# Cross-attention kernel on one core: second attention begun inside the batch loop, first stage reordered, unread products on TensorE

## The chip, the cores and the metric

The kernel runs on one core of a Trainium2 chip. Its time is the device time of one execution in microseconds (us). Three executions of the kernel before took 262.43, 263.16 and 263.74 us; their median, 263.16, is the time before. A profiled execution was recorded apart from them.

## What is computed

```python
# stage 0: only batch 0 matters (its attention is added to every batch)
q, k, v = x[0] @ Wq.T, ctx[0] @ Wk.T, ctx[0] @ Wv.T      # 256 tokens, 256 features, 16 heads of 16
tgt2 = softmax(q k^T / 4) v                               # per head
y = x + tgt2                                              # x: (32, 256, 256)
# stage 1: for each of 32 batches
nF, nX = layernorm(y) * w2 + b2, layernorm(ctx) * w1 + b1
attended = softmax(nF nX^T / 16) nX
h = gelu(attended @ fc1.T + fc1_b)                        # 4 hidden features
cross = h @ fc2.T + fc2_b
nc = layernorm(cross) * w3 + b3
self = softmax(nc nc^T / 16) nc                           # the second attention
out = nF + gamma2 * (cross + gamma1 * self)
```

## The kernel before

There are no helpers of a compiler here: each engine has its own hand-written program (functions under `@block.tensor`, `vector`, `scalar`, `gpsimd`, `sync`), and semaphores tie them together. So an instruction that waits holds back everything behind it on its engine, and the order of the lines is the order of the work.

**First attention** (VectorE L301 to L416, ScalarE L700 to L724, TensorE L811 to L903). 16 heads are done as eight pairs, `p = 0..7`. Per pair TensorE writes scores for two heads into two of four banks (L865), VectorE takes row maxima (L380), ScalarE four exponentials (L718), TensorE transposes them into banks 5 and 6 (L881), ScalarE copies bank 5 (L724) and VectorE bank 6 (L386), and every second pair TensorE multiplies with the values (L894). In the same loop VectorE takes the statistics of the first six context batches and, at `p = 6` and `p = 7`, sets the padding of `sU` to zero (L400, two memsets) and cuts the output operand in three bf16 parts (`output_operand`, L330, four chained instructions).

**Joint.** VectorE adds tgt2 to batches 0 and 1 (L468), GpSimd to all later ones (L615, `add`). Statistics (L351), then a reciprocal root on GpSimd (L622) and the normalization: y on VectorE (L371), context on GpSimd (L635).

**Loop over 32 batches** `b` (TensorE L965 on). Per batch: transposes of a later pair (`turned`, L852) into banks 3, 4, 2 in turn, evacuated by ScalarE into `XT` and `Fall` (L735, L738); scores of batch b (L915); maxima (L488); two exponentials (L762); transposes of the weights of b - 1 (L923), which ScalarE copies into PT (L756). Every four batches, a projection of the context to the four hidden features (L935), turned by way of a copy on VectorE (vT, L514) and L943, and the product of weights and values (`apply`, L953), turned back by way of oTq (VectorE, L522) and L961 (`apply_back`), saved in OA (L525). DMA loads run on one queue (SP), four pairs ahead.

**Algebra** (`algebra(g, part)`, L434). For each half `g` of the tokens (32 columns) VectorE runs a chain in which each instruction waits for the one before (`link`): reciprocal and bias, products with a 5 x 5 form and a reduction (L447), a reciprocal root by three Newton steps (L430 to L432), products with a 6 x 6 form (L460), and a cut into bf16 parts (L287 to L290). GpSimd cuts the other side (`right`, L667 to L675). `LATE` says after which batch each part of half 0 runs, `NEXT` after which iteration of the second attention each part of half 1 runs:

```python
LATE = {26: (0,), 29: (1,), 30: (2,), 31: (3,), 32: (4,), 33: (5,)}
NEXT = {0: (0,), 2: (1,), 3: (2, 3), 4: (4,), 5: (5,)}
```

The VectorE and TensorE loops run to b = 35; the steps behind batch 31 are the last transposed weights, `apply(7)` and `apply_back(7)`, and on VectorE the last parts of the algebra.

**Second attention** (TensorE L1077 on): 16 pairs of batches, `p = 0..15`, in a pipeline of 21 iterations. `turn(p)` (L1001) transposes both cut sides into bank 4; ScalarE copies it for even p (L775), VectorE for odd p (L542). `scores(p)` (L1012); VectorE takes maxima of two batches (L535); these are turned (L1023), copied by ScalarE (L781) and subtracted by TensorE (`shift`, L1031); ScalarE takes exponentials (L787). At even p: `attend` (16 products, L1044), `output_turn` (L1063); at odd p `back` (L1053). VectorE copies the result (L548), saves it (OB, L553), and GpSimd cuts it (L681 to L688). From p = 5 on, `output(p - 5)` (L1073) writes banks 6 and 7 and VectorE adds them to `Fall` (`finish`, L564); a pair of batches is then stored (SP, L270). The next `output` waits for that addition.

## Time and profile before

| | us |
|---|---|
| median of three executions | 263.16 (262.43 to 263.74) |
| the profiled execution, whole | 262.2 |
| its span, first to last instruction | 260.4 |
| busy: TensorE / weight loads | 213.0 / 143.4 |
| busy: VectorE | 207.4 |
| busy: ScalarE | 140.9 |
| busy: GpSimd | 125.4 |
| mean granted TensorE clock (share of full speed) | 0.854 |
| first attention | 0 to about 42 |
| loop over the batches | about 50 to 174 |
| second attention and output | about 178 to 260 |

Engines in the rows: PE is TensorE (PEld its weight loads, which overlap), DVE is VectorE, ACT ScalarE, POOL GpSimd, SP the engine that issues the DMAs. A row of the timeline gives the start, the duration, the engine and line, what is written and read, and how many instructions are merged; in brackets the idle time before it and what ended it. A busy TensorE may still be far from its peak, as its instructions overlap. The clock of TensorE has two levels, 2.4 GHz (1.00) and 1.2 GHz (0.50). The 16 pairs of stores end 3.2 us after the last addition.

### The profile page before, as it was taken

Reading aid. Unit: us, or ns where it says so; the run is one execution under the profiler, and the core shown is the slowest. Engines: PE = TensorE matmul, PEld = TensorE weight load, DVE = VectorE, ACT = ScalarE, POOL = GpSimd, SP = SyncE. Lnnn points to the kernel's source line nnn. Section 1 sums busy time; section 2 is a strip of 40 time slices with the busy share of each in tenths; the row PEclk is TensorE's granted clock in tenths of the full one; section 3 lists DMA queues with packets and bytes.
Section 4 is the critical chain, followed back from the end, with each engine's and each line's share of the span. In section 5 each row is a group of like instructions: output and inputs, shape, how many; then the busy total and the mean of one; then the engine's idle time right before and its main releaser. Section 6 shows DMA issues by size and latency. Waiting matters only on the chain.

```text
span 260.4 us, 4676 instructions
## 1 busy us (share of the span) xinstructions
PE 213.0 (82%) x1614; PEld 143.4 (55%) x1614; DVE 207.4 (80%) x413; ACT 140.9 (54%) x260; POOL 125.4 (48%) x186
## 2 busy tenths in 40 slices
PE   3989868289999999999999999963786568888731
PEld 3856535267778778796988789632222223333210
DVE  5678886999999989888998953886569958988663
ACT  1066764216677778586776778840564335454300
POOL 6000087677999979999697840041003512222220
PEclk9999999659999999999999999985555557777865
DMA  5980000044444425355450000000000024333556
GB/s 185 363 302 3 1 1 3 0 161 161 165 161 142 144 95 156 114 164 162 159 166 0 4 0 3 0 0 3 1 0 1 0 83 162 141 144 125 204 198 242
DMA packets 14711, 26.80 MB, mean 103 GB/s; under 512 B 1760, under 2 KB 1760, under 8 KB 14688
## 3 DMA queue, kind: packets, MB, share of 16 engines
q1 hardware_dynamic: 14688, 26.50, 29.2%
q8 instruction: 13, 0.21, 0.3%
q14 instruction: 10, 0.08, 0.1%
HBM read 18.11 MB, written 8.39 MB: 102 GB/s over the span
## 4 chain that ended last, share of the span: by engine, by line
PE 59%; DVE 24%; ACT 6%; issue 6%; POOL 2%; DMA 1%; SPq 0%; POOLq 0%; DVEq 0%; ACTq 0%
PE psum L915 17%; PE psum L852 8%; PE psum L923 5%; PE psum L1044 4%; DVE xN L371 4%; DVE nm L535 3%; DVE bn L351 3%; PE psum L953 3%; PE psum L822 2%; PE psum L935 2%; PE psum L1012 2%; DVE Fall L564 2%; PE psum L1073 2%; PE psum L865 2%; PE psum L881 2%
## 5 line engine op out<-in xcount | busy, mean ns | idle before, releaser
L915 PE MATMUL psum<-XT,Fall 128*128 128x256 f32 x256 | 62.6, 388 | 1.1 <-ACT Fall L738 1.1
L915 PEld LDWEIGHTS psum<-XT,Fall 128*128 128x128 f32 x256 | 47.2, 195 | 7.1 <-ACT Fall L738 1.7
L615 POOL TENSOR_TENSOR xN<-xN,tgt 128x512 f32<-128x512 f32 x30 | 39.1, 1306 | 1.5 <-DVE tgt L415 1.5
L635 POOL TENSOR_SCALAR cN<-cN,nmean,rstd 128x256 f32<-128x256 f32 x64 | 36.4, 579 | 2.4 <-POOL rstd L622 2.3
L371 DVE TENSOR_SCALAR xN<-xN,bn,rstd 128x256 f32<-128x256 f32 x64 | 34.8, 586 | 1.1 <-POOL rstd L622 1.1
L756 ACT ACTIVATE PT<-psum 128x512 f32<-128x512 f32 x32 | 19.1, 598 | 28.6 <-PE psum L923 28.6
L488 DVE TENSOR_REDUCE nmax<-psum 128x2 f32<-128x512 f32 x32 | 21.9, 684 | 12.6 <-PE psum L915 12.4
L622 POOL TENSOR_TENSOR rstd<-vps,minus_half 128x8 f32<-128x8 f32 (+1 forms) x16 | 24.8, 1549 | 13.8 <-DVE vps L362 13.8
L762 ACT ACTIVATE E<-psum,nmax 128x256 f32<-128x256 f32 x64 | 26.7, 473 | 8.3 <-DVE nmax L488 8.2
L681 POOL CAST sC<-co 128x160 bf16<-128x160 f32 x8 | 2.5, 317 | 53.9 <-DVE co L558 53.9
L738 ACT ACTIVATE Fall<-psum,par 128x512 f32<-128x512 f32 x32 | 23.4, 792 | 4.8 <-PE psum L852 4.7
L564 DVE TENSOR_TENSOR Fall<-psum,Fall 128x1024 f32<-128x1024 f32 x16 | 19.5, 1221 | 7.6 <-PE psum L1073 7.6
L735 ACT ACTIVATE XT<-psum,b1s,w1s 128x512 f32<-128x512 f32 x32 | 23.0, 788 | 3.7 <-PE psum L852 3.7
L535 DVE TENSOR_REDUCE nm<-psum 128x4 bf16<-128x1024 f32 x16 | 19.5, 1218 | 4.5 <-PE psum L1012 4.3
L351 DVE BATCH_NORM_STATS2 bn<-cN 128x6 f32<-128x512 f32 x32 | 22.2, 693 | 0.0
L852 PE MATMUL psum<-ident,xN 128*128 128x128 f32 x128 | 18.2, 289 | 4.7 <-DVE xN L371 4.7
L351 DVE BATCH_NORM_STATS2 bn<-xN 128x6 f32<-128x512 f32 x32 | 21.9, 685 | 0.0
L923 PE MATMUL psum<-ident,E 128*128 128x128 f32 x128 | 20.2, 280 | 1.6 <-ACT E L762 1.6
L787 ACT ACTIVATE PT<-psum 128x1024 f32<-128x1024 f32 x16 | 16.4, 1022 | 9.2 <-PE psum L1031 9.1
L923 PEld LDWEIGHTS psum<-ident,E 128*128 128x128 f32 x128 | 14.3, 141 | 9.6 <-issue 6.5
L852 PEld LDWEIGHTS psum<-ident,xN 128*128 128x128 f32 x128 | 15.7, 150 | 5.5 <-issue 5.1
L852 PE MATMUL psum<-ident,cN 128*128 128x128 f32 x128 | 17.1, 274 | 0.1
(156 smaller groups left out, 337.0 us busy)
## 6 DMA issues: line engine op xcount, KB each, us to landing
cN<-ctx SPq DMA_DIRECT2D x32, 256.0 KB, 2.9
xN<-x SPq DMA_DIRECT2D x32, 256.0 KB, 4.1
out<-Fall SPq DMA_DIRECT2D x32, 256.0 KB, 2.3
x0T<-x0t SPq DMA_DIRECT2D x1, 256.0 KB, 2.7
wqT<-wqt SPq DMA_DIRECT2D x1, 256.0 KB, 3.3
c0T<-c0t SPq DMA_DIRECT2D x1, 256.0 KB, 4.0
wkT<-wkt SPq DMA_DIRECT2D x1, 256.0 KB, 5.0
wvT<-wvt SPq DMA_DIRECT2D x1, 256.0 KB, 5.2
```

The costliest lines, as they stand in the source:

```text
L351: dve.bn_stats(bn[:, (b // 2) % 4, side, b % 2, :], src[:, b % SLOTS, :].rearrange("p (t d) -> p d t", t=NT)).then_inc(st_ok, 1)
L371: dve.tensor_scalar(own, own, stat(p, 1, m, t, 1), root_of(p, 1, m, t), ALU.subtract, ALU.mult)\
L535: dve.tensor_reduce(nm2[:, p % 2, :, 0:NT], scored(p).rearrange("p (m t k) -> p m t k", m=2, t=NT), AX.X, ALU.max, negate=True).then_inc(m ...
L564: dve.tensor_tensor(own, psum[:, 6 * 512:8 * 512], own, ALU.add).then_inc(fin_ok, 1)
L615: pool.tensor_tensor(xN[:, b % SLOTS, :], xN[:, b % SLOTS, :], tgt2[:, :, :].rearrange("p t d -> p (t d)"), ALU.add).then_inc(y_ok, 1)
L622: pool.tensor_tensor(rstd[:, p % 4, sides, :].rearrange("p s k -> p (s k)"), vps[:, p % 4, sides, :].rearrange("p s k -> p (s k)"), minus_ ...
L635: pool.tensor_scalar(own, own, nmean[:, p % 4, NT * m + t:NT * m + t + 1], root_of(p, 0, m, t), ALU.add, ALU.mult)\
L738: act.activation(Fall[:, 2 * p:2 * p + 2, c, :], tiles(own), ACT.Identity, bias=c_("b2", c), scale=c_("w2", c)).then_inc(evac_ok, 1)
L762: act.activation(E[:, b % 2, t * N:(t + 1) * N], bank[SBANK1[b % 3]][:, t * N:(t + 1) * N], ACT.Exp, bias=nmax[:, b % 2, t:t + 1]).then_in ...
L852: last = pe.transpose(bank[TBANK[n % 3]][:, m * N + t * P:m * N + (t + 1) * P], z[:, (2 * p + m) % SLOTS, t * D + c * P:t * D + (c + 1) * ...
L915: last = pe.matmul(bank[SBANK1[b % 3]][:, t * N:(t + 1) * N], Fall[:, b, c, t * P:(t + 1) * P], XT[:, p % 4, c, m * N:(m + 1) * N], start= ...
L923: last = pe.transpose(bank[SBANK1[b % 3]][:, k * N + t * P:k * N + (t + 1) * P], E[:, b % 2, t * N + k * P:t * N + (k + 1) * P], ident[:, :])
```

## The change

It does nine things.

1. The two memsets of `sU` go from `p = 6` of the first attention to the very start of VectorE's program, with a semaphore of their own.
2. The cuts of the output operand: part 1 goes behind the copies of Q and K, part 2 from `p = 7` to batch 18 of the loop.
3. ScalarE copies bank 5 (weights of the pair before) between the exponentials of the first and those of the second head, and TensorE waits for each half of the copies apart.
4. The additions of tgt2 to batches 2 and 3 go from GpSimd to VectorE, so VectorE does the first four; GpSimd starts its own at batch 4 and waits until VectorE has normalized batches 0 and 1.
5. In the loop the copies vT and oTq go from VectorE to ScalarE.
6. The algebra of half 0 is split in nine parts and runs in batches 20 to 29; the transposes `turn(0)`, `turn(1)` and `scores(0)` run in TensorE's batches 30 and 31. `apply(7)`, `apply_back(7)` and the saving of OA run inside iteration 0 of the second attention.
7. ScalarE makes all copies sT, even and odd.
8. `output(13)` and `output(15)` write to banks 2, 3 and 0, 1, which the scores no longer need. All additions stay on VectorE: the tuple `ASIDE`, which would send some by way of ScalarE to GpSimd, is empty, and the code around it makes no instructions.
9. `keep_busy(n, b)`: n products of the identity with itself, 128 columns wide, into a bank that is written anew before it is read. Seven at the start, eleven behind the first six context transposes, four and three around the last weights, then five behind each `shift` up to p = 4 and two from p = 5 on.

```diff
-LATE = {26: (0,), 29: (1,), 30: (2,), 31: (3,), 32: (4,), 33: (5,)}
-NEXT = {0: (0,), 2: (1,), 3: (2, 3), 4: (4,), 5: (5,)}
+LATE = {20: (0,), 22: (1,), 23: (2,), 24: (3,), 25: (4,), 26: (5,), 27: (6,), 28: (7,), 29: (8,)}
+NEXT = {0: (0,), 2: (1, 2), 3: (3, 4), 4: (5, 6), 5: (7, 8)}
+ASIDE = ()
...
+    def result(n):
+        return {13: (2, 3), 15: (0, 1)}.get(n, (6, 7))
...
+        for side in range(2):
+            dve.memset(sU[:, side, :, SU:SLOT], 0.0).then_inc(pads_ok, 1)
...
-        output_operand(1)
...
+        output_operand(1)
...
-                if p == 2 * EARLY:
-                    for side in range(2):
-                        dve.memset(sU[:, side, :, SU:SLOT], 0.0).then_inc(zero_ok, 1)
-                elif p > 2 * EARLY:
-                    output_operand(2)
...
+                dve.wait_ge(zero_ok, 6)
+                products(ha[:, G, :], Q[:, :], H + 1)
+            elif part == 2:
+                link(dve.tensor_reduce(w5, produced(H + 1), AX.X, ALU.add))
+            elif part == 3:
...
+            elif part == 4:
...
+            elif part == 5:
+                products(u[:, G, :], K[:, :], U)
+            elif part == 6:
+                link(dve.tensor_reduce(uK[:, G, :], produced(U), AX.X, ALU.add))
+            elif part == 7:
+                left_cut(uK[:, G, :], cut[:, G, 0:U], sU[:, 0, G, :], U)
...
-                left_cuts(uK[:, G, :], cut[:, G, 0:U], sU[:, 0, G, :], U)
+                left_rest(cut[:, G, 0:U], sU[:, 0, G, :], U)
...
+        def add(b):
...
+        add(0)
+        add(1)
...
-        statistics(2, 1)
+        add(2)
+        add(3)
...
+        statistics(2, 1)
...
+        def saved(q):
+            dve.wait_ge(ob_mm, q + 1)
+            dve.tensor_copy(OA[:, q, :, :, :], by_batch(bank[7][:, 0:N], H + 1)).then_inc(o_saved, 1)
+        for b in range(B):
...
-            if b % 4 == 1 and q < QUADS:
-                dve.wait_ge(vt_mm, q + 1)
-                if q >= 1:
-                    dve.wait_ge(vb_mm, q)
-                dve.tensor_copy(vT[:, :], bank[6][:, 0:N]).then_inc(vT_ok, 1)
+            maximum(b)
...
-                    dve.wait_ge(oq_mm, q)
-                    if q >= 2:
-                        dve.wait_ge(ob_mm, q - 1)
-                    dve.tensor_copy(oTq[:, :], bank[7][:, 0:N]).then_inc(oTq_ok, 1)
+                values(q)
...
-                dve.wait_ge(ob_mm, q)
-                dve.tensor_copy(OA[:, q - 1, :, :, :], by_batch(bank[7][:, 0:N], H + 1)).then_inc(o_saved, 1)
+                saved(q - 1)
...
+            if b == 18:
+                output_operand(2)
...
-        def turned(p):
-            dve.wait_ge(st_mm, p + 1)
-            if p >= 2:
-                dve.wait_ge(s2_mm, p - 1)
-            dve.tensor_copy(sT[:, 1, :], bank[4][:, 0:NT * P].bitcast(BF16)).then_inc(sT_ok[1], 1)
...
+            dve.tensor_tensor(pair(n), results(n), pair(n), ALU.add).then_inc(fin_ok, 1)
...
-        turned(1)
+        saved(QUADS - 1)
...
-            if p % 2 == 1 and p + 2 < PAIRS:
-                turned(p + 2)
...
-            if b == 2:
+            if b == 4:
...
+                pool.wait_ge(zy_ok, 4)
...
-        add(2)
-        add(3)
...
+                if m == 0 and p >= 1:
+                    act.wait_ge(p0_mm, 2 * p - 1)
+                    if p >= 4:
+                        act.wait_ge(o0_mm, (p - 4) // 2 + 1)
+                    act.activation(PT[:, 2 * ((p - 1) % 3), :], bank[5][:, :], ACT.Copy).then_inc(pt0_ok[0], 1)
+            if p == 5:
+                act.wait_ge(o0_mm, NHP // 4)
+                act.activation(oT[:, 0, :], bank[0][:, :], ACT.Copy).then_inc(oT_ok[0], 1)
...
-            if b == 28:
-                hidden(0)
...
+        def turned_values(q):
+            act.wait_ge(vt_mm, q + 1)
+            if q >= 1:
+                act.wait_ge(vb_mm, q)
+            act.activation(vT[:, :], bank[6][:, 0:N], ACT.Copy).then_inc(vT_ok, 1)
+        def applied(q):
+            act.wait_ge(oq_mm, q + 1)
+            if q >= 1:
+                act.wait_ge(ob_mm, q)
+            act.activation(oTq[:, :], bank[7][:, 0:N], ACT.Copy).then_inc(oTq_ok, 1)
...
+            act.activation(sT[:, p % 2, :], bank[4][:, 0:NT * P].bitcast(BF16), ACT.Copy).then_inc(sT_ok[p % 2], 1)
...
+            if b >= 1:
+                weights_copied(b - 1)
+            exponentials(b)
+            if b % 4 == 1:
+                turned_values(q)
+            if b % 4 == 2 and q >= 1:
+                applied(q - 1)
+            if b == 21:
+                hidden(0)
+            if b == 29:
+                act.wait_ge(r_mm, 1)
+                act.activation(RT[:, :], bank[4][:, 0:DC * P // 2].bitcast(BF16), ACT.Copy).then_inc(rt_ok, 1)
+            if b == 30:
+                turned(0)
+        weights_copied(B - 1)
+        turned(1)
...
+            if p == 0:
+                applied(QUADS - 1)
+            if p + 2 < PAIRS:
...
+        def keep_busy(n, b):
+            for _ in range(n):
+                pe.matmul(bank[b][:, 0:P], ident[:, :], ident[:, :], start=True, stop=True)
+        pe.wait_ge(consts, 4)
+        keep_busy(7, 4)
...
-                if p >= 2:
-                    pe.wait_ge(pt0_ok[0], p - 1)
-                    pe.wait_ge(pt0_ok[1], p - 1)
...
+                    if p >= 2:
+                        pe.wait_ge(pt0_ok[m], p - 1)
...
+        keep_busy(11, 7)
...
+            if p == 0:
+                pe.wait_ge(rt_ok, 1)
+                pe.wait_ge(pads_ok, 2)
+                pe.wait_ge(alg, ALG["left", 0])
+                pe.wait_ge(right_ok, 6)
+                pe.wait_ge(zero_ok, 6)
...
-            if p >= 2:
+            if p == 0:
+                pe.wait_ge(evac_ok, 4 * PAIRS)
+            elif p == 1:
+                pe.wait_ge(PT_ok, B)
+            else:
...
+            if n == 14:
+                pe.wait_ge(fin_ok, own_adds(13))
+            elif n in (13, 15):
+                pe.wait_ge(exp2_ok, PAIRS)
...
+            elif n >= 1:
+                pe.wait_ge(fin_ok, own_adds(n))
...
-        pe.wait_ge(alg, ALG["left", 0])
-        pe.wait_ge(right_ok, 6)
-        pe.wait_ge(zero_ok, 8)
-        pe.wait_ge(PT_ok, B)
-        pe.wait_ge(rt_ok, 1)
-        turn(0)
-        scores(0)
-        turn(1)
...
+            if b == 31:
+                scores(0)
+            if b == B:
+                pe.wait_ge(V1_ok, QUADS)
+                keep_busy(4, 6)
...
+            if b == 30:
+                turn(0)
+            if b == 31:
+                turn(1)
...
+            if p == 0:
+                keep_busy(3, 6)
+                apply(QUADS - 1)
...
+            if p == 0:
+                apply_back(QUADS - 1)
...
+                keep_busy(5 if p < 5 else 2, 5)
```

## Rows read from the trace of the kernel before

**Rows 1.** Windows: length, busy PE, PEld, DVE, ACT, POOL, granted clock, DMA share, GB/s.
```profile
110.00:120.00 10.00, 10.00 (x76) 8.35 (x75) 8.77 (x21) 7.59 (x15) 9.19 (x10) 1.00 0.56 175
160.00:170.00 10.00, 9.79 (x79) 7.17 (x78) 6.56 (x16) 8.34 (x16) 0.00 (x0) 1.00 0.01 2
200.00:210.00 10.00, 5.44 (x40) 1.84 (x32) 9.62 (x18) 2.41 (x5) 5.45 (x11) 0.50 0.05 20
230.00:240.00 10.00, 8.05 (x79) 3.09 (x81) 8.69 (x16) 5.18 (x9) 2.50 (x9) 0.79 0.42 157
```

**Rows 2.** Timeline, first attention (start, us, engine, line, [idle before]); last, the last score.
```profile
4.92 3.78 PE L822 MATMUL psum<-x0T,wqT 128*128 128x256 f32 x8 [0.47 <-DMA wqT<-wqt]
...
9.19 0.18 DVE L288 TENSOR_TENSOR Rcut<-Rt,stR 128x20 f32<-128x20 f32 x1
...
28.17 1.09 PE L881 MATMUL psum<-ident,E 128*128 128x128 f32 x8 [0.79 <-ACT PT L724]
...
33.55 1.74 DVE L400 MEMSET sU<- 128x896 uint32 x2
...
34.21 1.09 PE L881 MATMUL psum<-ident,E 128*128 128x128 f32 x8 [0.80 <-ACT PT L724]
...
37.16 0.45 DVE L288 TENSOR_TENSOR Rcut<-Rt,stR 128x20 f32<-128x20 f32 x1
...
168.49 1.95 PE L915 MATMUL psum<-XT,Fall 128*128 128x256 f32 x8
```

**Rows 3.** Timeline, joint between first attention and loop, and three rows from inside the loop.
```profile
43.78 2.37 DVE L468 TENSOR_TENSOR xN<-xN,tgt 128x512 f32<-128x512 f32 x2
...
48.71 2.31 DVE L371 TENSOR_SCALAR xN<-xN,bn,rstd 128x256 f32<-128x256 f32 x4 [0.54 <-POOL rstd L622]
...
130.34 1.27 POOL L615 TENSOR_TENSOR xN<-xN,tgt 128x512 f32<-128x512 f32 x1
...
135.07 0.72 DVE L371 TENSOR_SCALAR xN<-xN,bn,rstd 128x256 f32<-128x256 f32 x2
...
139.07 1.87 DVE L371 TENSOR_SCALAR xN<-xN,bn,rstd 128x256 f32<-128x256 f32 x2
```

**Rows 4.** Timeline, end of the loop: exponentials, transposes, products of the algebra.
```profile
143.07 0.84 ACT L762 ACTIVATE E<-psum,nmax 128x256 f32<-128x256 f32 x2
...
144.95 0.60 PE L923 MATMUL psum<-ident,E 128*128 128x128 f32 x4
...
164.38 0.98 DVE L424 TENSOR_TENSOR kv<-ha,Q 128x800 f32<-128x800 f32 x1
```

**Rows 5.** Window of four batches inside the loop.
```profile
118.46:133.30 14.84, 14.84 (x120) 12.12 (x124) 12.99 (x28) 10.65 (x21) 12.26 (x15) 1.00 0.44 144
```

**Rows 6.** Timeline, head of the second attention.
```profile
178.31 0.29 PEld L961 LDWEIGHTS psum<-ident,oTq 128*128 128x128 f32 x2 [3.91 <-DVE oTq L522]
...
180.77 1.23 DVE L535 TENSOR_REDUCE nm<-psum 128x4 bf16<-128x1024 f32 x1 [1.53 <-PE psum L1012]
...
185.98 1.23 DVE L535 TENSOR_REDUCE nm<-psum 128x4 bf16<-128x1024 f32 x1 [0.81 <-PE psum L1012]
```

**Rows 7.** Timeline, two iterations of the second attention, and late value products.
```profile
230.66 0.41 DVE L542 COPY sT<-psum 128x512 bf16<-128x512 bf16 x1
...
232.50 1.89 PE L1044 MATMUL psum<-PT,u 128*6 128x256 f32 x16
...
239.47 1.89 PE L1044 MATMUL psum<-PT,u 128*6 128x256 f32 x16
...
244.56 1.05 PE L1044 MATMUL psum<-PT,u 128*6 128x256 f32 x16 [0.31 <-ACT PT L787]
```

**Rows 8.** Window of 2 us inside an odd iteration.
```profile
230.00:232.00 2.00, 1.12 (x15) 0.54 (x13) 1.93 (x6) 1.09 (x2) 0.28 (x2) 1.00 0.70 262
```

**Rows 9.** Timeline, the last two additions.
```profile
254.00 1.22 DVE L564 TENSOR_TENSOR Fall<-psum,Fall 128x1024 f32<-128x1024 f32 x1 [0.79 <-PE psum L1073]
...
256.02 1.23 DVE L564 TENSOR_TENSOR Fall<-psum,Fall 128x1024 f32<-128x1024 f32 x1 [0.80 <-PE psum L1073]
```

More of the change, by code:

```diff
@@ L237, in score_bank, with own_adds, results, aside @@
         return bank[2 * (1 - p % 2) + m]
+    def own_adds(n):
+        return sum(i not in ASIDE for i in range(n))
+    STORED = tuple(range(PAIRS))
+    def result(n):
+        return {13: (2, 3), 15: (0, 1)}.get(n, (6, 7))
+    def results(n):
+        a, _ = result(n)
+        return psum[:, 512 * a:512 * (a + 2)]
+    def aside(n):
+        return XT[:, (n // 2) % 2, :, :].rearrange("p c n -> p (c n)")
+    def pair(n):
+        return Fall[:, 2 * n:2 * n + 2, :, :].rearrange("p b c n -> p (b c n)")
     TURNS = [(p, 0) for p in range(EARLY)] + [(p, 1) for p in range(EARLY)] \
@@ L454, in algebra @@
                 newton(v, y, t)
-            elif part == 3:
+            elif part == 4:
                 newton(v, y, t)
@@ L576, in _ @@
                 returned((p - 3) // 2)
-            if p >= 5:
+            if p >= 5 and p - 5 not in ASIDE:
                 finish(p - 5)
@@ L688, in output_cuts, with add_aside @@
             pool.tensor_tensor(to[:, :, 2 * CO:3 * CO], left, to[:, :, CO:2 * CO], ALU.subtract).then_inc(sC_ok, 1)
+        def add_aside(n):
+            pool.wait_ge(aside_ok, ASIDE.index(n) + 1)
+            pool.tensor_tensor(pair(n), aside(n), pair(n), ALU.add).then_inc(added_ok, 1)
         right(0)
@@ L695, in _ @@
                 output_cuts((p - 3) // 2)
+            if p - 5 in ASIDE:
+                add_aside(p - 5)
     @block.scalar
@@ L707, in _ @@
         for p in range(NHP + 1):
[L708 to L712 removed]
+            for m in range(2):
+                if p < NHP:
                     act.wait_ge(max0_ok, 2 * p + m + 1)
@@ L794, in output_turned, with set_aside @@
             act.activation(cT[:, q % 2, :], bank[4][:, 0:NT * P].bitcast(BF16), ACT.Copy).then_inc(cT_ok, 1)
-        turned(0)
-        for p in range(2 * QUADS + 3):
+        def set_aside(n):
+            act.wait_ge(f_mm, n + 1)
+            if ASIDE.index(n) >= 2:
+                act.wait_ge(added_ok, ASIDE.index(n) - 1)
+            act.activation(aside(n), results(n), ACT.Copy).then_inc(aside_ok, 1)
+        for p in range(2 * QUADS + 4):
             if p < PAIRS:
                 maxima_turned(p)
-            if p % 2 == 0 and p + 2 < PAIRS:
+            if p == 0:
+                applied(QUADS - 1)
+            if p + 2 < PAIRS:
                 turned(p + 2)
@@ L803, in _ @@
                 weights(p)
+            if p - 5 in ASIDE:
+                set_aside(p - 5)
             if p == 1:
@@ L1072, in output @@
                     rows = slice(SLOT * m, SLOT * m + SC)
-                    last = pe.matmul(bank[6 + m][:, c * N:(c + 1) * N], RT[rows, c * P:(c + 1) * P],
+                    last = pe.matmul(bank[result(n)[m]][:, c * N:(c + 1) * N], RT[rows, c * P:(c + 1) * P],
                                      cT[rows, (n // 2) % 2, (n % 2) * N:(n % 2 + 1) * N], start=True, stop=True)
             last.then_inc(f_mm, 1)
-        pe.wait_ge(alg, ALG["left", 0])
-        pe.wait_ge(right_ok, 6)
-        pe.wait_ge(zero_ok, 8)
-        pe.wait_ge(PT_ok, B)
-        pe.wait_ge(rt_ok, 1)
-        turn(0)
-        scores(0)
-        turn(1)
+        for b in range(B + 1):
+            k, m, q = b // 2, b % 2, b // 4
+            if k + 1 < PAIRS and (m == 1 or k + 1 >= EARLY):
+                turned(k + 1, m)
+            if b < B:
+                score(b)
+            if b % 4 == 1 and q < QUADS:
+                project(q)
+            if b % 4 == 2:
+                project_back(q)
+                if q >= 1:
+                    apply(q - 1)
+            if b % 4 == 3 and q >= 1:
+                apply_back(q - 1)
+            if b == 31:
[3 more added lines that the diff above has]
+                keep_busy(4, 6)
+            if b >= 1:
+                weights_turned(b - 1)
+            if b == 29:
+                pe.wait_ge(evac_ok, 62)
+                pe.wait_ge(alg, ALG["stR"])
+                for c in range(DC):
+                    last = pe.transpose(bank[4][:, c * P // 2:(c + 1) * P // 2].bitcast(BF16),
+                                        stR[:, c, :, :].rearrange("p m r -> p (m r)"), identb[:, :])
+                last.then_inc(r_mm, 1)
+            if b == 30:
+                turn(0)
+            if b == 31:
+                turn(1)
         for p in range(2 * QUADS + 5):
```

124 lines of the change are left out of this document (41 added, 83 removed).

## The prediction

> **What bounds the kernel now.** I read the stretches first, then each joint between stages in the timeline. The stretches [rows 1] show three regimes. Inside the loop (58 to 170 us) TensorE is busy 9.8 to 10.0 of every 10 us at full clock (2.4 GHz), so there only work on TensorE, or an engine that falls behind it, moves the end. From 200 to 210 us it is busy 5.44 of 10 at a granted clock of 0.50 (1.2 GHz), and VectorE 9.62: latencies and VectorE set the pace. After 214 us the clock alternates between its levels (mean 0.79 from 230 to 240). Ahead of the loop the time goes in chains between engines.
>
> **Start and first attention.** The 16 projection products (8 then 8) run on the path: the first eight took 3.78 us, while eight such products took 1.95 in the loop [rows 2]. The change puts seven unread products in front. If that brings the full clock 1.5 us earlier the second set gains most of 1 us, if not nothing. Ends 0 and 1.8; I take 0.7, as the first set still runs cold.
> The two memsets (33.55 to 35.29) hold back a row maximum whose scores were finished before they began; at VectorE's start they lie in its wait for the parameters [rows 2]. Gain 1.7.
> ScalarE copied half of the turned weights after all four exponentials; TensorE's transposes at 34.21 waited 0.80 for that copy [rows 2]. Two iterations last 34.21 - 28.17 = 6.04 [rows 2]: transposes 1.1, value products 1.0, scores 1.1, first maximum 0.7, exponentials 1.57, copy 0.5. With the copy before the second pair and the two waits split, the first transposes hide behind the second exponentials: about 0.4 less per two iterations, 3.5 times, 1.4. Ends 0 and 2. The operand cuts moved to batch 18 gain nothing here (VectorE then waited anyway); those put behind K fit the wait for the first scores.
>
> **Joint to the loop.** Two additions go from GpSimd to VectorE, two instructions more there. But VectorE's own two took 2.37 us while GpSimd added, and its four normalizations 2.31 beside another GpSimd addition; two normalizations beside a GpSimd power took 0.72, beside additions 1.87 [rows 3]. With GpSimd made to wait for the first four normalizations I count: additions 1.2 (gain 1.2), two more additions 1.2 that fill the wait for the root, normalizations 1.45 (gain 0.9). About 2.0, and 0.3 from the first score, which ran at half clock and may run warm after eleven unread products. Gain 2.3; ends 1 and 3.5. First stage and joint: 6.1.
>
> **Loop.** The algebra of the first half moves from batches 26 to 33, where VectorE was busy 6.56 of 10 us [rows 1], to 20 to 29, and a cut to batch 18. Up to batch 25: cuts 0.85, reciprocal and bias 1.0, products 1.0 [rows 4], reduction 1.0, eight small instructions 2.0, seven more 1.7: 7.5 us. VectorE is busy 12.99 of the 14.84 us of four batches [rows 5], idle 1.9, so 3.8 in eight, and the copies of vT and oTq (0.42 each, four of them) leave it: 5.5. Exponentials were ready at 143.9 for transposes at 144.95 [rows 4], elsewhere 2 us ahead: a maximum may come some 1.5 us later. That leaves 0.5 us of stall if the moved instructions keep their length. They lose their quiet neighbour, though: GpSimd was at 0 between 160 and 170 us, and works 9.2 of 10 here [rows 1]. A cut beside GpSimd's normalizations took 0.45, like two of its neighbours, and the same one beside an idle GpSimd 0.18 [rows 2]: +0.3 each. Some 21 of the moved ones are of kinds that would meet it; GpSimd's powers do not disturb (0.72 above) and are a fifth of its time, so I take 0.2 each, 4.2. Stall 4.7, ends 0 and 10; with the turn of pair 0 now ahead of the last score, 0.35: a loss of 5.0. ScalarE takes the 0.42 copies with room (7.59 of 10 busy) [rows 1]. Its two table loads for Gelu only move from batch 28 to 21.
>
> The Trainium skill (SBUF — State Buffer, Who interferes with whom) says that a VectorE instruction with two SBUF inputs and a GpSimd instruction that reads SBUF exclude each other for the whole instruction. By it each would wait out the rest of a GpSimd addition (1.27 long [rows 3]), not a part of 0.3; that is the third rival below.
>
> **Head of the second attention.** Before, the last score ended at 170.4; then came the last weights, the last value products, the cuts, and maxima(0) at 180.77, maxima(2) at 185.98: 15.6 us after it [rows 2, 6]. Between lay a wait of 3.91 of TensorE's queue for a copy (L522) that stood behind the algebra on VectorE. After, by the same durations from the end T of the last score: scores(0) T+0.5, maxima(0) T+1.0, last exponentials T+2.0 (they queue behind one copy on ScalarE), their copy T+4.1, last value products T+4.2 to 5.2, back T+5.8, OA saved T+6.4, maxima(1) T+7.6, weights(0) T+8.1, maxima(2) T+8.7. VectorE now waits for OA before maxima(1), and every turned(p) queues on ScalarE between two others. Gain 15.6 - 8.7 = 6.9; half clock would cost 1.4 of it. From p=3 to p=6 VectorE runs without a gap (algebra of the second half, same instructions), so each odd turned() that leaves it (0.41, some 0.33 in the chain) counts: p=1, 3, 5, 7, 1.4 in all. At p=6 the path goes through TensorE: value products 1.89 cold, 1.05 warm [rows 7], 0.8 less. Gain 6.9 + 1.4 + 0.8 = 9.1.
> The unread products cost some 0.12 us each (half of a 256-column product, 1.95 / 8 [rows 2]), cold twice that. I count those of the head (four and three) and the five an iteration up to p=4 at nothing: TensorE waits there for exponentials, for a copy or for a maximum, 1 us or more. Without that cover they are 0.6 to 1.2 an iteration, and TensorE itself is late next.
>
> **Steady part, p=8 to 15.** Two iterations take 7.0 us (232.50 to 239.47) [rows 7]: finish 1.1, maximum 1.15, turned 0.33, OB copied 0.3, then TensorE from the maxima's transpose to the output, 4.1. Without turned: -0.33. TensorE's part holds the 16 value products (1.89 at 1.2 GHz, 1.05 at 2.4) and two sets of four (some 0.2 each): 1.2 less if the clock stays up, and two unread products more, 0.25 warm or 0.5 cold. So per pair of iterations between +0.1 and -1.1 (VectorE's own 5.9 us is the floor). The granted clock was 0.79 here before [rows 1]: full in the odd iterations, where TensorE was busy 1.1 of 2 us [rows 8], and down again after them. I take -0.6, four times: 2.4. Ends 0 and 4.4.
>
> **End.** The last three additions stood 2.02 apart: addition (1.23), output products that wait for it, addition. With other banks for two of them they follow each other in 1.23, the last transfer as before 3.2 after it: 2 x 0.8 = 1.6 [rows 9], less 0.2 as the transfers, 2 us a pair, close up. Gain 1.4. All other additions stay where they are: ASIDE is empty, so the aside code makes nothing.
>
> **Sum.** -6.1 + 5.0 - 9.1 - 2.4 - 1.4 = -14.0. The profiled execution took 262.2 (span 260.4), so 248.2; the runs' median, 263.16, is 1.0 above that execution, so 249. A measurement of this kernel tells about 0.5% (1.3 us) from no change.
>
> **Rivals.**
> *Clock and cover both hold*: TensorE stays at 2.4 GHz through the second attention and VectorE keeps up. The loop loses 1.4 and not 5.0, the steady part gives 4.4, the start 1.8: 6.7 less, 242. For it: unread products fill gaps like that of [rows 8]. Against: from p=5 on they are only two, 0.25 us in some 3. 0.2.
> *The clock does not hold and VectorE lags*: head loses 1.4, p=6 0.8, steady gives 0, loop 10 instead of 5, start 0: 10.3 more, 258 to 259; half of it 254. For it: from 200 to 210 us the clock stayed at 0.50 though TensorE was busy 5.44 of 10 [rows 1]. 0.22 for 252 to 259.
> *Slower than before*: the moved algebra, batches 18 to 25, each of 21 instructions waiting out a whole GpSimd addition of 1.27: 7.5 + 27 - 5.5 - 1.5 = 27 of stall instead of 4.7, 271. It turns slower from 0.9 us per instruction on. Against: the cuts that met GpSimd paid 0.3. 0.04.
> *It does not begin in the loop*: turn(0) waits for the cuts of either engine. GpSimd's (4.2 us, after its last normalization at 152.7) and VectorE's (end in batch 29) are both ready before batch 30, but a lag of VectorE of over 4 us would move them: the head's 6.9 shrink to 3, 253. 0.04.
> My forecast, a small stall and a clock that alternates: 0.5.
>
> **Range and chances.** The own ends of the terms give 240 to 259; holding 8 in 10 and leaving out the slower case and the worst of the second rival, 242.5 to 256. Faster by over 0.5%: 0.93; within: 0.03; slower: 0.04.
>
> **What would show it.** Right: no memset before a maximum in the first attention; VectorE's first additions at about 0.6 each; maxima(0) about 1 us after the last score and maxima(2) under 9; last additions 1.23 apart. The loop step is right if the batches 22 to 26 show TensorE waiting for exponentials and VectorE's small instructions at 0.3 to 0.5; wrong if TensorE stays at 10.00 there, or if it stalls over 10. The clock step is wrong if the steady cycle stays near 6.7 or falls to 5.9. The whole is wrong if the loop loses what the head gains.

## The result and the profile after

The changed kernel takes 246.95 us (median of four executions, 246.19 to 247.89); the kernel before took 263.45 (262.43 to 263.82) beside it. The ratio is 0.938, with a 95% interval from 0.934 to 0.942. The profiled execution took 246.86, its span is 245.1 and the mean granted clock 0.957 (before: 262.2, 260.4, 0.854).

The windows of the changed kernel (columns as in [rows 1]), first those that answer to [rows 1], then the two that differ most:

```profile
110.00:120.00 10.00, 10.00 (x88) 7.76 (x87) 8.31 (x18) 6.69 (x14) 9.64 (x11) 1.00 0.33 112
160.00:170.00 10.00, 9.75 (x84) 7.19 (x76) 3.49 (x8) 5.40 (x14) 0.00 (x0) 1.00 0.01 2
230.00:240.00 10.00, 5.04 (x50) 1.97 (x46) 6.90 (x12) 1.19 (x2) 3.00 (x10) 0.70 0.56 210
...
190.00:200.00 10.00, 5.05 (x37) 2.54 (x38) 9.53 (x14) 2.79 (x6) 5.20 (x11) 0.65 0.15 54
200.00:210.00 10.00, 9.68 (x95) 4.86 (x96) 6.19 (x10) 5.45 (x10) 1.51 (x5) 0.84 0.28 104
210.00:220.00 10.00, 9.40 (x101) 5.12 (x98) 9.37 (x15) 6.62 (x13) 2.43 (x9) 1.00 0.44 160
```

The loop is nearly as full as before: between score(6) and score(31) TensorE is busy 92.56 of 93.72 us (before: 92.09 of 92.30). The second attention, at 0.50 and 0.79 in [rows 1], now runs at 2.4 GHz except from 193.1 to 203.3 us and from 234.0 to the end. Before, the clock was at half speed from 174.3 to 215.3 and then alternated.

The starts of nine events cut both spans into stretches. Measured from the timelines, us:

| stretch | before | after | difference | forecast |
|---|---|---|---|---|
| start to first scores | 13.07 | 11.14 | -1.93 | -0.7 |
| to the last value products | 26.93 | 24.10 | -2.83 | -3.1 |
| to score(6) | 36.19 | 35.72 | -0.47 | -2.3 |
| to score(31) | 92.30 | 93.72 | +1.42 | +5.0 |
| to maxima(2) | 17.49 | 10.58 | -6.91 | -6.9 |
| to maxima(7) | 24.23 | 23.32 | -0.91 | -1.4 |
| to finish(1) | 4.14 | 5.09 | +0.95 | -0.8 |
| to finish(9) | 28.14 | 24.35 | -3.79 | -2.4 |
| to finish(13) | 9.49 | 9.95 | +0.46 | 0 |
| to the end | 8.42 | 7.13 | -1.29 | -1.4 |
| sum | 260.4 | 245.1 | -15.3 | -14.0 |

The timeline of the changed kernel at the start and at the end, which answers to [rows 2] and [rows 9]:

```profile
1.90 3.36 PE L873 MATMUL psum<-ident 128*128 128x128 f32 x14 [1.90 <-POOL ident L608]
...
5.55 1.97 PE L888 MATMUL psum<-x0T,wqT 128*128 128x256 f32 x8
...
237.97 3.49 DVE L586 TENSOR_TENSOR Fall<-psum,Fall 128x1024 f32<-128x1024 f32 x3 [1.61 <-PE psum L1130]
```

Seven unread products are 14 instructions and 3.36 us, and the first projections behind them take 1.97 instead of 3.78. The last three additions follow each other at 1.14 us.

### The profile page after: what moved, and what is told of

Same layout as the page of the kernel before. It is cut to its first block, busy times and chain, and to the rows that moved or that the text cites. A ratio compares the mean times of both kernels' runs of the same rounds, so it can differ in the third digit from the quotient of the medians.

```text
span 245.1 us, 4980 instructions
## 1 busy us (share of the span) xinstructions
PE 214.2 (87%) x1758; PEld 154.2 (63%) x1758; DVE 198.0 (81%) x391; ACT 148.9 (61%) x284; POOL 124.4 (51%) x184
## 4 chain that ended last, share of the span: by engine, by line
PE 55%; DVE 28%; issue 8%; ACT 4%; POOL 2%; DVEq 0%; POOLq 0%; ACTq 0%
PE psum L981 15%; PE psum L918 7%; DVE bn L381 6%; DVE xN L401 6%; PE psum L989 5%; PE psum L873 5%; DVE nm L564 3%; PE psum L1019 3%; PE psum L1095 3%; PE psum L931 2%; DVE nmax L524 2%; PE psum L1001 2%; PE psum L946 2%; PE psum L959 2%; PE psum L888 2%
## 5 line engine op out<-in xcount | busy, mean ns | idle before, releaser
L981 PE MATMUL psum<-XT,Fall 128*128 128x256 f32 x256 | 60.9, 381 | 1.8 <-ACT Fall L763 1.8
L981 PEld LDWEIGHTS psum<-XT,Fall 128*128 128x128 f32 x256 | 46.1, 190 | 7.2 <-ACT Fall L763 2.2
L656 POOL TENSOR_SCALAR cN<-cN,nmean,rstd 128x256 f32<-128x256 f32 x64 | 38.5, 614 | 2.4 <-POOL rstd L643 2.3
L636 POOL TENSOR_TENSOR xN<-xN,tgt 128x512 f32<-128x512 f32 x28 | 35.7, 1278 | 1.6 <-DVE xN L401 1.6
L401 DVE TENSOR_SCALAR xN<-xN,bn,rstd 128x256 f32<-128x256 f32 x64 | 33.8, 571 | 0.7 <-POOL rstd L643 0.7
L793 ACT ACTIVATE E<-psum,nmax 128x256 f32<-128x256 f32 x64 | 26.8, 475 | 10.9 <-DVE nmax L524 10.9
L524 DVE TENSOR_REDUCE nmax<-psum 128x2 f32<-128x512 f32 x32 | 22.0, 686 | 13.7 <-PE psum L981 13.2
L643 POOL TENSOR_TENSOR rstd<-vps,minus_half 128x8 f32<-128x8 f32 (+1 forms) x16 | 25.0, 1564 | 15.4 <-DVE vps L392 15.3
L873 PE MATMUL psum<-ident 128*128 128x128 f32 x144 | 23.3, 308 | 1.9 <-POOL ident L608 1.9
L873 PEld LDWEIGHTS psum<-ident 128*128 128x128 f32 x144 | 19.4, 208 | 5.5 <-issue 3.6
L918 PE MATMUL psum<-ident,xN 128*128 128x128 f32 x128 | 17.1, 274 | 2.6 <-DVE xN L401 2.3
```

The source lines that it names most:

```text
L401: dve.tensor_scalar(own, own, stat(p, 1, m, t, 1), root_of(p, 1, m, t), ALU.subtract, ALU.mult)\
L524: dve.tensor_reduce(nmax[:, b % 2, :], tiles(bank[SBANK1[b % 3]]), AX.X, ALU.max, negate=True)\
L636: pool.tensor_tensor(xN[:, b % SLOTS, :], xN[:, b % SLOTS, :], tgt2[:, :, :].rearrange("p t d -> p (t d)"), ALU.add).then_inc(y_ok, 1)
L643: pool.tensor_tensor(rstd[:, p % 4, sides, :].rearrange("p s k -> p (s k)"), vps[:, p % 4, sides, :].rearrange("p s k -> p (s k)"), minus_ ...
L656: pool.tensor_scalar(own, own, nmean[:, p % 4, NT * m + t:NT * m + t + 1], root_of(p, 0, m, t), ALU.add, ALU.mult)\
L793: act.activation(E[:, b % 2, t * N:(t + 1) * N], bank[SBANK1[b % 3]][:, t * N:(t + 1) * N], ACT.Exp, bias=nmax[:, b % 2, t:t + 1]).then_in ...
```

## The experiments

**Unread products.** Three kernels leave out all of them (`no_unread`), the seven at the start (`no_start`), or those behind the shifts (`no_second`):

```diff
 no_unread
-            for _ in range(n):
+            for _ in range(0):
 no_start
-        keep_busy(7, 4)
 no_second
-                keep_busy(5 if p < 5 else 2, 5)
```

> The changed kernel without any of its unread products. Theory: they keep TensorE's clock up in three places, worth 1.9 us at the start (first scores from 11.1 back to 13.1 us), nothing in the loop, and some 3 us in the second attention (cycle of two iterations from 6.13 back to 6.7 or 7.0 us): 251 to 252.5 us. Rival: they cost about what they give beyond the start, since five of them take 1.2 us: 248 to 249 us.

> The changed kernel without the seven products at the start. Theory: the projections ran at half clock before and at full clock after, so the first scores start again at about 13.1 us and the whole takes 1.9 us more, 248.9 us; everything behind keeps its distances. Rival: the second projection waits for its transfers anyway (wkT lands at about 7.3 us), so little over half of it comes back: 248.0 us or less.

> The changed kernel without the products behind each shift in the second attention (those at the start and around the head stay). Theory: the clock alternates again, the 16 value products take 1.89 us in some iterations, and the cycle from finish(1) to finish(9) goes from 24.35 to about 26.8 us: 249 to 250 us. Rival: without them TensorE also saves 0.52 us in each even iteration, where it is on the path, and the cycle stays near 6.1 to 6.3 us: 246.5 to 247.5 us.

Measured: `no_unread` 250.65 (248.73 to 250.94; ratio 0.952, 0.946 to 0.957); `no_second` 248.46 (247.48 to 249.54; 0.946, 0.940 to 0.952); `no_start` 249.7, with executions of 247.8, 248.2, 251.3 and 254.9 (ratio of the three shorter ones 0.947, 0.939 to 0.955). So all unread products together are worth 3.7 us, and 12 to 13 us of the change have nothing to do with them. `no_unread` is just below its theory. `no_start` is too scattered to decide: one of its executions is in the rival's range, one between rival and theory, and two are well above both. `no_second` lies between its theory and its rival (finish(1) to finish(9) takes 25.65; the theory had 26.8), and its executions overlap with those of the changed kernel. In the traces of `no_start` and `no_unread` the first scores begin at 12.94 and 13.04; with the seven products they begin between 11.05 and 11.92 in nine traces, at 11.14 in that of the changed kernel. That term is real, but the spread of the executions of `no_start` was not foreseen. The windows of `no_unread`:

```profile
190.00:200.00 10.00, 5.02 (x38) 1.89 (x31) 9.59 (x18) 2.71 (x5) 5.46 (x11) 0.50 0.09 35
200.00:210.00 10.00, 10.00 (x78) 3.57 (x79) 6.71 (x9) 5.84 (x9) 1.51 (x5) 0.50 0.28 106
```

Without them the clock is at half speed from 177.9 to 212.1 and finish(1) to finish(9) takes 27.55, near the 28.14 of before. The clock is down from 44.8 to 55.1 as well, and yet the joint takes 35.69, as in the changed kernel (35.72): the eleven products there gave nothing.

**Additions back on GpSimd.**

```diff
-            elif b < 4:
+            elif b < 2:
                 dve.wait_ge(y_first, b + 1)
             else:
-                dve.wait_ge(y_ok, b - 3)
+                dve.wait_ge(y_ok, b - 1)
...
-        add(2)
-        add(3)
+        statistics(2, 1)
         normal(0)
         normal(1)
-        statistics(2, 1)
...
-            if b == 4:
+            if b == 2:
                 pool.wait_ge(tgt2_ok, 2 * NT)
-                pool.wait_ge(zy_ok, 4)
...
+        add(2)
+        add(3)
         root(0)
```

> The changed kernel with the additions of batches 2 and 3 back on GpSimd and its wait removed. Theory (from the trace after): the joint gained only 0.5 us by moving them, so 247.2 to 247.8 us; VectorE's own additions take 1.2 us each again and its first four normalizations 2.3. Rival (the forecast's term): moving them was worth 2.0 us, 249 us.

Measured: 258.5 (256.5 to 260.4); ratio of the three shorter ones of four 0.980 (0.971 to 0.989): far outside of both expectations. Its profiled execution is the longest of the four, 260.4. From the first scores to score(6) it needs 62.11 us instead of 59.82, so the additions are worth 2.3 there. The rest is one stretch, finish(1) to finish(9): 35.29 instead of 24.35. Its windows and two rows of its timeline:

```profile
200.00:210.00 10.00, 8.91 (x59) 4.42 (x59) 5.14 (x9) 4.00 (x6) 0.33 (x1) 0.50 0.29 107
210.00:220.00 10.00, 10.00 (x68) 4.68 (x64) 5.75 (x9) 4.27 (x7) 1.50 (x5) 0.50 0.28 105
220.00:230.00 10.00, 10.00 (x66) 4.68 (x65) 5.75 (x9) 4.27 (x7) 1.50 (x5) 0.50 0.29 107
```

```profile
212.05 1.22 PE L872 MATMUL psum<-ident 128*128 128x128 f32 x4
213.21 1.89 PE L1094 MATMUL psum<-PT,u 128*6 128x256 f32 x16
```

At 1.2 GHz TensorE is the bound: two unread products take 1.22, 16 value products 1.89 (0.71 and 1.05 in the changed kernel), and two iterations 9.9 instead of 6.1. The clock had fallen at 194.1 and rose again only at 235.1. Three runs take this apart.

`adds_gpsimd_only` is the same kernel without the products behind the shifts (47 of them; the expectation counts 39):

> The changed kernel with additions 2 and 3 back on GpSimd, and without the 39 unread products (two instructions each) that stand behind the shifts of the second attention. The kernel with those products and the same two additions on GpSimd was 258.5 us: 2.6 us of its loss over the changed kernel stand before score(6), and 11 us stand in the second attention, where the granted clock was 0.50 in 200 to 220 and TensorE was busy 18.9 of 20 us. Theory (the 11 us are the unread products at half clock, not the additions): 248.5 us of the kernel without the products, plus 2.5 us in the joint = 250 to 252 us. Rival (the two additions themselves cost more than the joint, whatever TensorE does in the second attention): 256 to 259 us.

Measured: 250.3 (248.0 to 252.9). The theory holds: with the same additions, leaving unread products out saves 8 us. They are dear once the clock is low.

`shifted` makes only the joint longer:

```diff
+        for k in range(2):
+            link(dve.tensor_tensor(big[:, 512 * k:512 * (k + 1)], tgt2..., tgt2..., ALU.mult))
         add(2)
...
-        keep_busy(11, 7)
+        keep_busy(21, 7)
```

> The changed kernel with two extra element-wise products of 128x512 on VectorE in the joint (into memory that nothing reads before it is written again; 1.3 us each by the row of the addition, so 2.6 us), and ten more unread products ahead of the first scores so that TensorE doesn't rest in the time that this adds. Nothing else is changed, so the whole of the loop and of the second attention comes some 2.5 us later. Theory (the clock's course in the second attention depends on when that part runs, and the unread products cost twice at the lower level): the granted clock falls for longer than the 10 us of the changed kernel, and the time is 254 to 259 us. Rival (the shift alone does nothing further; the loss of the kernel with two additions on GpSimd had its cause in the additions): 247 plus 2.5 = 249 to 250 us.

Measured: 248.2 (247.9 to 251.0), ratio 0.944 (0.938 to 0.950); finish(1) to finish(9) 24.28. My theory fell, though the test is weaker than it was meant to be: first scores to score(6) grew by 0.95 and not 2.6, and maxima(7) starts 1.6 us later than in the changed kernel, against 2.4 in `adds_gpsimd`. A start 1.6 us later does not bring the long stretch at half clock.

**Filling the gaps around the fall of the clock.** In the changed kernel TensorE rested 2.11 us at 189.3 and 2.31 at 196.3, and the granted clock was 0.50 from 193.1 to 203.3. Only the first rest lies ahead of the fall:

```profile
191.41 0.22 PE L1074 MATMUL psum<-identb,nm 128*64 128x128 bf16 x1 [2.11 <-DVE wqT L571]
...
198.65 0.58 PE L1048 MATMUL psum<-identb,sU 128*128 128x128 bf16 x4 [2.31 <-issue]
...
199.70 1.22 PE L873 MATMUL psum<-ident 128*128 128x128 f32 x4
200.85 1.89 PE L1095 MATMUL psum<-PT,u 128*6 128x256 f32 x16
```

```diff
 filled
         if p == QUADS:
+            keep_busy(6, 4)
...
-                keep_busy(5 if p < 5 else 2, 5)
+                keep_busy(5 if p < 7 else 2, 5)
...
             if p >= 5:
                 output(p - 5)
+            if p == 4:
+                keep_busy(5, 6)
```

> The changed kernel with more unread products where the granted clock fell in its second attention: 5 behind the first output turn (TensorE rested 2.11 us there at 189.3), 5 in place of 2 behind the shifts 5 and 6, and 6 ahead of the wait for the second half's algebra in turn(8) (TensorE rested 2.31 us there at 196.3). Theory: the clock stays at 1.00 in 190 to 204, which gives back the 0.95 us that maxima(7) to finish(1) grew by and some of the step before it: 245.3 to 246.3 us. Rival (the clock falls all the same, or the products stand in the way of the shifts): 247 to 249 us.

Measured: 245.79 (245.57 to 246.04), ratio 0.933 (0.929 to 0.936). The same place in its timeline, and the window:

```profile
199.71 1.38 PE L873 MATMUL psum<-ident 128*128 128x128 f32 x10
201.02 1.05 PE L1096 MATMUL psum<-PT,u 128*6 128x256 f32 x16
```

```profile
190.00:200.00 10.00, 7.01 (x65) 5.06 (x64) 9.69 (x15) 2.97 (x7) 5.45 (x11) 1.00 0.15 54
```

The clock stays at 2.4 GHz there and maxima(7) to finish(1) takes 3.73 instead of 5.09. The two rests were filled together, so which of them matters is not shown. Then the same filling under the kernel that had lost 11 us, `adds_gpsimd_filled`:

> The kernel filled (the changed kernel with more unread products in 189 to 199 us of its trace; 245.8 us, granted clock 1.00 there) with additions 2 and 3 back on GpSimd. On the changed kernel the same edit cost 11.5 us: 2.6 up to score(6), 10.9 between finish(1) and finish(9), where the clock was at half speed and TensorE never rested. Theory (those 10.9 us are the price of the clock that fell at 194 us, and the products keep it from falling): 245.8 plus 2.3 to 2.8 = 248.1 to 248.6 us, finish(1) to finish(9) 24 to 25 us. Rival (the additions on GpSimd bring the second attention to half clock whatever TensorE does before): 254 to 259 us.

Measured: 248.2 (247.8 to 248.5), ratio 0.945 (0.940 to 0.949); finish(1) to finish(9) 24.28. The theory holds: the additions cost 2.4 us, and the 11 us were the clock's. The intervals of `filled` and of the changed kernel touch, but none of their executions overlap (the longest of `filled` is 246.04, the shortest of the other 246.19).

**First stage alone**, on the kernel before:

```diff
-                if p == 2 * EARLY:
-                    for side in range(2):
-                        dve.memset(sU[:, side, :, SU:SLOT], 0.0).then_inc(zero_ok, 1)
-                elif p > 2 * EARLY:
-                    output_operand(2)
...
+                if m == 0 and p >= 1:
+                    act.wait_ge(p0_mm, 2 * p - 1)
...
+                    act.activation(PT[:, 2 * ((p - 1) % 3), :], bank[5][:, :], ACT.Copy).then_inc(pt0_ok[0], 1)
```

> The kernel before with the first stage's part of the change alone: VectorE's two memsets at the start instead of in batch pair 6, the two cuts of the output operand moved behind the operand products and to batch 26, ScalarE's copies of the weights ahead of the second two exponentials and its one output copy a step earlier, and TensorE's waits for the copies split. Additions and everything behind stay as before. Theory: 3.1 us by the forecast's terms (1.7 and 1.4), 2.8 by the trace (the last value products came 26.93 us behind the first scores before and 24.10 after), all of it carried to the end: 260 to 261 us. Rival (the gain is taken back in the joint, where GpSimd's additions wait for the arrival of the inputs or the clock falls): 262.5 to 264 us.

Measured: 261.48 (259.79 to 262.99), ratio 0.993 (0.989 to 0.996). First scores to last value products takes 24.08, so the first stage gains its 2.85; but first scores to score(6) takes 62.08 against 63.12, a gain of 1.04 only. The whole gains 2.2 us by the medians and 2.4 in the trace, with 1.1 of it ahead of the first scores (at 11.93 instead of 13.07). That is not this edit's: `algebra_in_loop`, whose start is that of the kernel before, has its first scores at 11.91; in both traces the clock rose at 8.3 to 8.5 us and not at 10.5. The joint takes 1.8 back. Its timeline:

```profile
34.09 6.87 POOL L634 TENSOR_SCALAR cN<-cN,nmean,rstd 128x256 f32<-128x256 f32 x12
40.93 2.48 POOL L614 TENSOR_TENSOR xN<-xN,tgt 128x512 f32<-128x512 f32 x2
...
39.79 4.17 DVE L465 TENSOR_TENSOR xN<-xN,tgt 128x512 f32<-128x512 f32 x2
```

VectorE's two additions take 4.17, against 2.37 in [rows 3]. Before, GpSimd had finished its twelve normalizations when they came; now they arrive earlier, beside the last of those and both of GpSimd's additions. The same place in the changed kernel:

```profile
39.02 1.75 DVE L499 TENSOR_TENSOR xN<-xN,tgt 128x512 f32<-128x512 f32 x2
42.10 1.29 DVE L499 TENSOR_TENSOR xN<-xN,tgt 128x512 f32<-128x512 f32 x2
43.71 1.38 DVE L401 TENSOR_SCALAR xN<-xN,bn,rstd 128x256 f32<-128x256 f32 x4 [0.31 <-POOL rstd L643]
45.26 1.28 POOL L636 TENSOR_TENSOR xN<-xN,tgt 128x512 f32<-128x512 f32 x1 [1.59 <-DVE xN L401]
```

Away from GpSimd's normalizations two additions take 1.29; GpSimd's first comes after VectorE's normalizations. The Trainium skill (SBUF — State Buffer, Who interferes with whom) has a VectorE instruction with two SBUF inputs and a GpSimd instruction that reads SBUF exclude each other; the 4.17 against 1.29 agrees.

**Algebra in the loop alone**, on the kernel before:

```diff
-LATE = {26: (0,), 29: (1,), 30: (2,), 31: (3,), 32: (4,), 33: (5,)}
+LATE = {20: (0,), 23: (1,), 24: (2,), 25: (3,), 26: (4,), 28: (5,)}
...
-            if b == 28:
+            if b == 21:
                 hidden(0)
```

> The kernel before with the first half's algebra alone moved: its six parts behind batches 20, 23, 24, 25, 26 and 28 instead of 26, 29 to 33, and the Gelu behind batch 21's exponentials instead of 28's; no turn, score, copy or addition of the second attention comes earlier. Forecast's reading: VectorE's queue in the loop is the bound, so the loop from score(6) to score(31) grows by about 5 us, and the head gives some of it back: 263 to 267 us. Rival, by the trace of the changed kernel (GpSimd starves while VectorE works at the algebra, and only the Gelu's table loads show, 1.1 us): the loop grows by 1 to 1.5 us and the head loses the VectorE time of the parts that stood behind the last batch: 260 to 263 us.

Measured: 260.96 (257.76 to 263.93); ratio of the seven shorter ones of its ten executions 0.992 (0.988 to 0.997). score(6) to score(31) takes 94.13 in its trace, against 92.30: 1.8 us, near the rival and far from 5. To maxima(2) it takes 15.27 instead of 17.49. The rival has the time right but not the cause: TensorE's waits here are for exponentials whose maxima stood behind the algebra, and none is at the Gelu's table loads (136 to 141 us).

```profile
145.17 1.34 DVE L448 TENSOR_TENSOR W<-W,ha 128x160 f32<-128x160 f32 x1
...
149.72 0.66 PE L923 MATMUL psum<-ident,E 128*128 128x128 f32 x4 [0.40 <-ACT E L762]
...
161.92 0.66 PE L923 MATMUL psum<-ident,E 128*128 128x128 f32 x4 [0.82 <-ACT E L762]
```

The multiplication of 1.34 takes 0.32 in the kernel before; a GpSimd addition ran beside it from 145.05 to 146.33. Ahead of the second wait VectorE worked 2.8 us at the products with the 6 x 6 form and their reduction. So what the forecast feared for the loop does happen, at about a third of its size.

**The Gelu.** In the changed kernel TensorE waited once for what the table loads delayed:

```profile
135.07 1.28 ACT L793 ACT_TABLE_LOAD   x1
...
137.53 0.44 PE L1027 MATMUL psum<-ident,oTq 128*128 128x128 f32 x2 [0.91 <-ACT oTq L780]
```

```diff
+            if b == 21:
+                hidden(0)
             if b >= 1:
                 weights_copied(b - 1)
             exponentials(b)
...
-            if b == 21:
-                hidden(0)
```

> The changed kernel with ScalarE's first Gelu ahead of batch 21's copy of the turned weights instead of behind its exponentials: ScalarE rested 1.50 us ahead of that copy (at 129.67 in the trace of the changed kernel), and the Gelu's input was ready at 128.24. Theory (the two table loads of 1.28 us each are what TensorE waited 0.91 us for at 137.53): one of them falls into the rest, the wait is gone, and the time is 245.7 to 246.3 us. Rival (the copy of the weights and the exponentials behind it come later by 1 us, and TensorE waits for those): 247 to 248 us.

> The edits of filled and gelu_placed together. Theory: 245.8 minus 0.9 = 244.6 to 245.2 us. Rival (the loop's gain is lost in the head, where TensorE waits for VectorE's maxima, or brings the clock down): 245.8 to 248 us.

Measured: the wait for oTq is gone, but a new one of 0.53 stands some five us earlier; score(6) to score(31) takes 93.30 instead of 93.72, so 0.4 and not 0.9. `gelu_placed` took 246.97 and 247.18 us in two executions (ratio 0.941, 0.934 to 0.947: the rival's range, and no gain over the changed kernel) and 258.47 and 258.55 in the two others. Its profiled execution is one of the short ones, with the clock at 0.72 in 190 to 200 (0.65 in the changed kernel). `filled_gelu`, with the gaps filled, took 245.52 (245.17 to 245.66, six executions; ratio 0.935, 0.931 to 0.939), between its theory and its rival. It has the lowest median of the study, but its executions overlap with those of `filled` (245.57 to 246.04). Its slowest execution is below the fastest of the changed kernel, though the intervals of the two ratios overlap.

## Why the prediction was right, and where its steps were not

The total, 249.0, is 2 us above 246.95. The largest step, the head, was right in mechanism and size; the others were less good, and that their errors nearly cancelled was luck.

- **Start**: right in kind, low in size. Taken 0.7 because the first projections were thought to run cold; they ran at 1.97, with the clock up at 5.3 us and not at 10.5, and the term is 1.9 between the two traces (1.8 by `no_start`). It depends on when the clock rises: the start of the kernel before took 13.07 in one trace and 11.91 in another, so by these traces the seven products bring anything from nothing to 2 us.
- **First attention**: 3.1 forecast, 2.83 measured, 2.85 alone.
- **Joint**: the step failed as a sum. The additions bring 2.3, as forecast (`adds_gpsimd`, 2.29), but only against a joint that the faster first stage had made 1.8 us worse. I priced them from [rows 3], where VectorE's two additions cost 2.37; that price was for additions that came after GpSimd's normalizations, and the first stage moved them into these (4.17). Even in the changed kernel the first two took 1.75, beside the last normalization, and only the later two 1.29. First stage and additions together gave 3.3 (2.83 + 0.47), not 5.4. The 0.3 for a warm first score came to nothing (35.69 in `no_unread`, 35.72 with the eleven products).
- **Loop**: 5.0 forecast, 1.42 measured (1.8 alone). TensorE's rests grew from 0.21 to 1.16 us and its work by 0.5, most of it the turn of pair 0. The failed step is the 4.2 us for moved instructions that meet GpSimd. The timeline of the changed kernel, VectorE at batch 18 and in batches 24 and 25, then GpSimd:

```profile
119.20 1.19 DVE L310 TENSOR_TENSOR Rcut<-Rt,stR 128x20 f32<-128x20 f32 x1
...
142.86 0.31 DVE L476 TENSOR_TENSOR W<-W,ha 128x160 f32<-128x160 f32 x1
...
144.20 0.19 DVE L455 TENSOR_TENSOR t<-r 128x32 f32<-128x32 f32 x1
...
146.50 0.17 DVE L392 TENSOR_SCALAR vps<-bn 128x8 f32<-128x8 f32 x1
```

```profile
141.66 1.13 POOL L656 TENSOR_SCALAR cN<-cN,nmean,rstd 128x256 f32<-128x256 f32 x2
146.75 1.65 POOL L643 TENSOR_TENSOR rstd<-vps,minus_half 128x8 f32<-128x8 f32 x1 [3.96 <-DVE vps L392]
```

  Most small instructions keep their quiet length of 0.18 to 0.19: while VectorE works at them, GpSimd has finished what it had and rests 3.96 us for the statistics that stand behind them. But where GpSimd still has work, they do meet. The cut at 119.20 takes 1.19 instead of 0.18, inside a GpSimd addition that ran from 119.09 to 120.36; one at 148.72, beside normalizations, took 0.45. Added up against their quiet lengths, all moved instructions grew by about 2.1 us, half of it in that one cut, while VectorE was idle for 13.2 us of the stretch. TensorE lost only 0.25 us behind VectorE, at 148.46 to a late maximum, and 0.91 to the Gelu's table loads. The third rival (271) counted 21 instructions that each wait out an addition; the rows show one that did, which is what the Trainium skill's rule (SBUF — State Buffer, Who interferes with whom) says of such a pair, and the others mostly found GpSimd at rest.
- **Head**: 6.91 against 6.9, by the durations of rows and the order of the queues. Before, VectorE worked from 171.25 to 177.80 at algebra ahead of the copy for which TensorE waited; now none of it stands there. The last score of the changed kernel and the maxima of pairs 0, 1 and 2:

```profile
164.68 1.95 PE L981 MATMUL psum<-XT,Fall 128*128 128x256 f32 x8
...
167.38 1.22 DVE L564 TENSOR_REDUCE nm<-psum 128x4 bf16<-128x1024 f32 x1
...
172.96 1.22 DVE L564 TENSOR_REDUCE nm<-psum 128x4 bf16<-128x1024 f32 x1
...
175.26 1.23 DVE L564 TENSOR_REDUCE nm<-psum 128x4 bf16<-128x1024 f32 x1 [0.17 <-PE psum L1063]
```

  From the score's end they come 0.8, 6.3 and 8.6 us later; forecast were 1.0, 7.6 and 8.7. No run makes this step alone: the algebra in the loop by itself brings 2.2 of it (`algebra_in_loop`), the rest is read from the traces.
- **To maxima(7)**: 0.91 against 1.4.
- **p = 6**: +0.95 against -0.8. I had taken the value products there as warm (1.05); they ran at 1.89, since the clock fell at 193.1, behind a rest of TensorE that the change had left open. With the rest filled the stretch is 3.73, a gain of 0.41.
- **Steady part**: 3.79 against 2.4; the cycle fell from 7.0 to 6.1 with all value products at 1.05. That the clock held here was the first rival's condition, to which I had given 0.2; its other half, the start, came true as well. Its loop of 1.4 did too. What kept the total from its 242 is the joint and p = 6.
- **End**: 1.29 against 1.4.
- **Unread products**: priced at 0.12 us each, they cost double, since each is two instructions (ten in 1.19 to 1.38 us at 2.4 GHz, four in 1.22 at 1.2). The x8 of the score row of 1.95 in [rows 2] are four products and not eight (and the projections four and four), which is where the price was halved. Their cover held, so nothing changed.

Errors of +3.6 (loop) and +2.6 (start, steady part) stood against -1.8 (joint), -1.8 (p = 6) and -1.3 (others and the last stretches): but for 1.3 us they cancelled.

**Open**: why the clock, once down at 193 to 194 us, comes back after some 10 us in the changed kernel and after 41 in `adds_gpsimd`, whose TensorE was busy 10.00 of 10 from 210 on. A busy TensorE is not needed for the long stretch: in the kernel before the clock was down for 41.0 us too, from 174.3, with TensorE busy 26.9 of them. A start 1.6 us later does not bring it (`shifted`), and one kernel does both (`gelu_placed`). Shown is only that it does not arise where the clock does not fall at that place.

## What to carry to other kernels

A term priced from the trace of before holds for the company its instructions had there: when an earlier step moves them in time, look again at what the neighbour on the shared memory does then, and don't add the gains. Where one engine feeds the other, they are rarely at work together, so check who feeds whom before charging contention to every instruction; the few that do meet can cost a whole instruction of the neighbour (1.19 us instead of 0.18). Unread products that keep TensorE's clock up are worth having where it waits, but look for the rests that they leave open: each product costs nearly double once the clock is down, and a set can lose more than it gave. Those behind the shifts gave 1.5 us (`no_second`, within the spread) and lost 8 (`adds_gpsimd` against `adds_gpsimd_only`).

## What was not expected of the hardware

With the same instructions, a kernel can run in 247 or in 258.5 us (`gelu_placed`). Its short executions have a mean granted clock of 0.952 and 0.944, its long ones 0.894 and 0.901; the long ones have no trace, so that they spent the difference at 0.50 in the second attention, as `adds_gpsimd` did, is an inference. The kernels whose clock holds at 1.00 through 190 to 210 us (`filled`, `filled_gelu`, `adds_gpsimd_filled`) spread over less than 0.8 us; those with products behind the shifts whose clock falls there over 1.7 to 11.6 (1.7 in the changed kernel, 7 in `no_start`, 11.6 in `gelu_placed`). Also new was that VectorE's additions of 128x512 vary from 0.65 us each alone to 2.09 beside GpSimd.
